# Context ahead of x, shared block sums, unstacked first maxima and products of zeros in the prologue of a gated cross-attention block

## The chip, the cores and the metric

One core of one Trainium2 chip runs the whole kernel. The metric is the device time in microseconds of one execution, as the median of several. TensorE multiplies, VectorE and ScalarE (ACT) work on its PSUM results, POOL (GpSimd) works on SBUF alone, and SyncE (SP), ACT and POOL issue the transfers. Each engine takes its own instructions strictly in order and waits on semaphores.

## The reference

The layer is computed for four batches of 512 rows and 512 columns, in fp32. `quant` below is per 1x128 block for the activations and per 128x128 block for the context.

```python
# attention to the context, as a product of two quantised matrices (fp8, with block scales)
x = x + tanh(g_xattn) * einsum('emk,enk->emn', quant_1x128(layernorm(x)), quant_128x128(ctx))
# causal self-attention, 16 heads of 32
h = layernorm(x)
fused = h @ (Wa * col_scale)          # 512 x 1536: q 24 + 8 tail, k 24 + 8 tail, v
q_tail, k_tail = where(w_rec > 0.1, swapped low-rank parts, low-rank parts)
attn = softmax(causal(q @ k.T / sqrt(32)))
x = x + tanh(g_ffn) * ((attn @ v) @ Wp)
```

## The kernel before

**Precision.** Each fp32 product is made of three fp32r products of high and low parts (hi hi, hi lo, lo hi), so a product of 512x512x128 takes 12 matmuls (L594 to L596). The quantised tiles are split into three fp8 parts and turned by 12 small products each (`turn_parts`, L610).

**Stages of a batch n.** Context: maxima over its blocks (`ctx_maximum`, t), two small transposes with the block scales (A, or B in the prologue for the next batch), POOL scales and clips (`scale_up`, s in the prologue, g in the body), ACT casts into fp8 parts (`cast`, C or c), TensorE turns (W). x: statistics (x), inverse deviation on POOL (i), normalisation (L), block maxima (F, or m), scales, again scale_up (u), cast (C) and turn (X). Then 16 block products (`partial_sum`, S, i is the row tile and k the block, number 4i+k), each added to x by VectorE with a scale of its own (`add_sum`, four operations of 128x128, L1201). Then second statistics (b), POOL's inverse deviation (r), ACT's normalisation (N), TensorE's turn (H), ACT's copy of the high part and VectorE's subtraction for the low part (H), and products q, k, v in four groups of heads (q0, k0, q1, k1, V0 to V3 or v3, Q2, K2, Q3, K3; a suffix .012 names the parts).

**The attention** runs in eight steps of two heads (u), software-pipelined: `max` (units 0 to 5, scores for the maxima of step u+1 on TensorE, L717, and masked maxima on VectorE, L1230), `rowmax` (L723, turns the maxima) with ACT's `neg` and a transfer into q_stack, `exp` (scores again, L734, and exponentials on ACT), POOL's `zero`, `pv` (values of step u-1, L748, which waits for the previous `norm` and for POOL), ACT's `copy`, TensorE's `back` (L757) and VectorE's `norm`. The rows of q and k, high and low, are stacked on 96 partitions by transfers (`stack_rows`, L345), so that one matmul makes all three products.

**What sets the order.** Every engine's order is written out by hand as strings of names: PE_STEPS, ACT_STEPS, DVE_STEPS, POOL_STEPS for batches 0 to 2, the _LAST strings for batch 3, the _END strings between batches and the _FIRST strings for the prologue. A name in a string is one piece on that engine; a piece late in one queue holds up everything behind it. `BEFORE` names the piece that must have freed a PSUM bank.

**The prologue** (the _FIRST strings) also prepares the weights: ACT rounds them (a, b), VectorE sorts the low-rank tails (T), POOL subtracts the rounded parts (j for q and k, l for v). q0 waits for all four j (`s_wlo`), v0 for all four l. The first x goes through `first_x`, which lies in qk_lo; the fourth part of the weights is loaded into qk_hi. SP loads x, then the context, then the weights. ACT issues eleven small transfers (gates, w_rec, col_root) before its first instruction. POOL_FIRST is `i0 s0 s1 ... s5 o0 s6 j0 s7 r0 j1 l0 l1 r1 l2 l3 r2 r3 j2 j3 ...`.

**Maxima of step 0.** They take the stacked rows: TensorE's M0 to M2 (two units each) wait for the transfers of q_stack and k_stack.

## Time and profile before

| | us |
|---|---|
| median of 3 runs | 502.21 |
| lowest, highest | 500.25, 502.68 |
| the profiled execution | 499.74 |
| its span, first to last instruction | 497.9 |
| TensorE busy | 440.6 (88%) |
| VectorE busy | 340.3 (68%) |
| ACT busy | 255.7 (51%) |
| POOL busy | 151.1 (30%) |

The span of the profiled execution is 1.8 us shorter than its time. The page's slices show TensorE filled from about 50 us on; the first 80 us are the prologue, then come four batches. Durations of matmuls are modelled to their ends and overlap, so the distance from one start to the next is the pace.

### The profile page before, as it was taken

To read this page: it belongs to the slowest core of one execution; us is meant where nothing else is said; L and a number is where in the kernel's file an instruction comes from. 1 tells how busy PE (TensorE), PEld (TensorE's weight loads), DVE (VectorE), ACT (ScalarE), POOL (GpSimd) and SP (SyncE) were. 2 spreads that over 40 slices of the span, in tenths; PEclk is the share of its full clock that TensorE was granted. 3 is DMA by queue.
4 is the path that set the end of the run, shared out by engine and by line. 5 is a ranking of instruction groups with operands and counts; after the bars stand their busy time and mean duration, and the time that the engine had idled before them with its cause. 6 is when DMAs were issued, how large, how long until landed. Compare 5 with 4: busy or idle time off the path is not lost.

```text
span 497.9 us, 7913 instructions
## 1 busy us (share of the span) xinstructions
PE 440.6 (88%) x2536; PEld 317.1 (64%) x2536; DVE 340.3 (68%) x1122; ACT 255.7 (51%) x498; POOL 151.1 (30%) x278
## 2 busy tenths in 40 slices
...
GB/s 225 197 1 87 39 246 82 91 69 96 146 2 2 89 101 193 67 56 95 141 27 0 64 97 127 138 53 98 97 11 2 58 102 97 64 95 102 60 21 86
DMA packets 27929, 42.62 MB, mean 86 GB/s; under 512 B 8272, under 2 KB 8528, under 8 KB 27888
## 3 DMA queue, kind: packets, MB, share of 16 engines
...
q0 software_dynamic: 192, 0.39, 0.3%
...
## 4 chain that ended last, share of the span: by engine, by line
PE 66%; DVE 24%; ACT 3%; issue 3%; DMA 2%; POOL 1%; SPq 0%; ACTq 0%; DVEq 0%; POOLq 0%
PE pv_bank L748 13%; DVE x_all L1201 10%; PE mm_bank L594 9%; PE mm_bank L595 8%; PE mm_bank L596 8%; PE exp_bank L734 6%; PE max_bank L717 5%; DVE max_bank L1230 5%; PE mm_bank L775 2%; PE mm_bank L777 2%; PE mm_bank L776 2%; PE turn_bank L610 2%; DVE bn L1208 2%; PE pv_bank L757 1%; DMA x_all<-in_x 1%
## 5 line engine op out<-in xcount | busy, mean ns | idle before, releaser
L1230 DVE CUSTOM_DVE_ANT_0 max_bank<-max_bank,causal 128x512 f32<-128x512 f32 (+3 forms) x256 | 121.0, 512 | 52.5 <-PE max_bank L717 52.0
L1002 ACT ACTIVATE work<-exp_bank 128x512 f32<-128x512 f32 (+1 forms) x192 | 94.9, 526 | 56.2 <-PE exp_bank L734 55.2
L512 POOL TENSOR_SCALAR_AFFINE_SELECT work<-work 128x384 f32<-128x384 f32 x64 | 33.4, 522 | 281.6 <-ACT work L1002 281.6
L748 PE MATMUL pv_bank<-work,v_aug 128*33 128x256 f32 (+3 forms) x512 | 78.9, 451 | 0.6 <-DVE work L1241 0.2
L734 PE MATMUL exp_bank<-q_stack,k_stack 97*128 97x512 f32 (+3 forms) x256 | 71.2, 341 | 7.6 <-ACT work L1002 6.5
L717 PE MATMUL max_bank<-k_stack,q_stack 96*128 96x512 f32 (+3 forms) x256 | 71.1, 338 | 2.4 <-DVE row_max L1230 1.8
L1201 DVE SCALAR_TENSOR_TENSOR x_all<-mm_bank,coef,x_all 128x128 f32<-128x128 f32 x224 | 61.5, 342 | 0.3
L748 PEld LDWEIGHTS pv_bank<-work,v_aug 128*33 128x33 f32 x512 | 29.7, 113 | 50.1 <-issue 42.1
L734 PEld LDWEIGHTS exp_bank<-q_stack,k_stack 97*128 97x128 f32 x256 | 45.6, 188 | 23.4 <-ACT work L1002 14.7
L594 PE MATMUL mm_bank<-xt_hi,w_hi 128*128 128x512 f32 x128 | 53.4, 417 | 0.7 <-ACT v_aug L981 0.7
L717 PEld LDWEIGHTS max_bank<-k_stack,q_stack 96*128 96x128 f32 x256 | 45.2, 191 | 12.7 <-DVE row_max L1230 3.7
L595 PE MATMUL mm_bank<-xt_lo,w_hi 128*128 128x512 f32 x128 | 50.3, 393 | 0.0
L596 PE MATMUL mm_bank<-xt_hi,w_lo 128*128 128x512 f32 x128 | 50.1, 392 | 0.0
L1213 DVE SCALAR_TENSOR_TENSOR qk_lo<-mm_bank,col_root,qk_hi 128x512 fp32r<-128x512 f32 x32 | 24.0, 749 | 34.0 <-ACT qk_hi L973 33.9
L973 ACT ACTIVATE qk_hi<-mm_bank,col_root 128x512 fp32r<-128x512 f32 x32 | 21.9, 686 | 32.6 <-PE mm_bank L596 32.6
L1230 DVE DVE_READ_ACCUMULATOR2_ANT row_max<- 128x1 f32 x256 | 36.1, 141 | 0.0
L996 ACT ACTIVATE values<-pv_bank 97x512 f32<-97x512 f32 x32 | 19.1, 598 | 27.4 <-PE pv_bank L748 27.4
L610 PE MATMUL turn_bank<-part_sign,tile_buf 128*128 128x128 fp8e4 x312 | 23.1, 227 | 5.4 <-ACT tile_buf L963 4.6
L642 PE MATMUL mm_bank<-wt_hi,wt_lo 128*128 128x512 f32 x56 | 23.3, 458 | 4.9 <-DVE x_all L1201 3.0
L596 PEld LDWEIGHTS mm_bank<-xt_hi,w_lo 128*128 128x128 f32 x128 | 24.0, 188 | 5.5
L594 PEld LDWEIGHTS mm_bank<-xt_hi,w_hi 128*128 128x128 f32 x128 | 24.2, 189 | 5.1 <-issue 1.2
L989 ACT ACTIVATE neg_max<-exp_bank 8x128 fp32r<-8x128 f32 x32 | 8.3, 260 | 35.5 <-PE exp_bank L723 35.5
...
## 6 DMA issues: line engine op xcount, KB each, us to landing
q_stack<-qk_hi SPq DMA_DIRECT2D x128, 64.0 KB, 2.0
...
```

The costliest lines, as they stand in the source:

```text
L512: pool.affine_select(out=three, in_=three, compare_op=ALU.is_ge, fill=0.0, base=0, pattern=[[0, 3], [1, P]], channel_multiplier=-1)
L594: pe.matmul(dst, l_hi(k), r_hi(k), start=(k == 0), stop=False)
L595: pe.matmul(dst, l_hi(k), r_lo(k), start=False, stop=False)
L596: last = pe.matmul(dst, l_lo(k), r_hi(k), start=False, stop=(k == NK - 1))
L610: last = pe.matmul(bank[:, P * k:P * k + P], part[:, P * k:P * k + P], part_sign[:, t, :], start=(t == 0), stop=(t == 2))
L717: last = pe.matmul(bank[:, col:col + width], q_stack[0:96, s, j, P * i:P * i + P], k_stack[0:96, s, j, 0:width], start=True, stop=True)
L734: last = pe.matmul(bank[:, col:col + T - P * i], k_stack[0:97, s, j, P * i:P * i + P], q_stack[0:97, s, j, P * i:T], start=True, stop=True)
L748: last = pe.matmul(pv_bank[64 * j:64 * j + D + 1, P * m:T], v_aug[:, m, 2 * u + j, :], prob[j][:, PROB_COL[m]:PROB_COL[m] + T - P * m], st ...
L1002: act.activation(prob[j][:, UNIT_COL[k]:UNIT_COL[k] + UNIT_LEN[k]], exp_bank[(3 * j + k) % 2][:, 0:UNIT_LEN[k]], ACT.Exp, scale=SCALE).the ...
L1201: last = dve.scalar_tensor_tensor(x_part, sum_bank(first, i, k)[:, P * t:P * t + P], coef[:, i, t, k:k + 1], x_part, ALU.mult, ALU.add)
L1213: dve.scalar_tensor_tensor(qk_lo[:, g % 2, w, :], mm_bank[w][:], col_root[:, g:g + 1], qk_hi[:, g % 2, w, :].bitcast(FP32), ALU.mult, ALU. ...
L1230: last = dve.tensor_tensor_reduce(max_bank[unit % 2][:, col:col + width], max_bank[unit % 2][:, col:col + width], causal[:, T - width:T], ...
```

## The change

It rewrites the prologue and puts the pieces of every step string into another order.

- SP loads the context before x; the fourth part of the weights comes in three pieces into other places (raw_v and raw_low early, raw_qk after the first j); the transfers of col_root are issued by SP behind the weights; ACT issues w_rec and the gates after its signs.
- `first_x` lies in v_aug; the maxima of first_x (F) are separate and the scales are made for two tiles at once (G).
- The context's turned parts are copied by VectorE (`first_ctx`, f) and not by ACT.
- Of the four block sums of a row tile, the fourth is multiplied by its scale on ACT (`first_product`, s) and added by POOL (a); VectorE adds three.
- Maxima of step 0 take q and k unstacked from qk_hi and qk_lo on 32 partitions, three matmuls for each product (`first_scores`), unit by unit.
- TensorE multiplies `causal[:, 0:384]`, which holds zeros, into exp_bank[1] (w0 to w11, four matmuls each).
- All step strings are in a new order, without a change to what is computed.

```diff
-    "max0 rowmax max1 S0 S1 pv max2 S2 max3 X1 max4 exp0 S3 back S4 exp1 exp2 S5 S6 max5 X2 exp3 exp4 exp5",
-    "rowmax max0 max1 S7 pv max2 max3 S8 S9 exp0 max4 exp1 back exp2 exp3 exp4 max5 X3 exp5 S10",
-    "S11 max0 rowmax max1 pv S12 max2 S13 max3 H0 S14 exp0 exp1 max4 exp2 H1 exp3 exp4 S15 exp5 max5 back",
-    "max0 rowmax max1 A0 pv exp0 H2 max2 exp1 exp2 max3 max4 exp3 exp4 max5 exp5 back",
+    "max0 X0 max1 rowmax S0 S1 max2 pv S2 max3 exp0 max4 S3 exp1 X1 back max5 exp2 S4 exp3 exp4 X2 exp5 S5 S6",
+    "max0 rowmax max1 S7 pv exp0 max2 S8 exp1 max3 exp2 max4 S9 X3 S10 exp3 exp4 max5 exp5 back",
+    "rowmax S11 max0 max1 S12 pv exp0 max2 S13 exp1 back max3 exp2 S14 H0 exp3 max4 exp4 max5 exp5 S15",
+    "H1 max0 rowmax max1 A0 pv exp0 max2 exp1 H2 exp2 max3 exp3 max4 exp4 max5 exp5 back",
...
-    "neg C1 copy X1 C2 exp0 exp1 exp2 exp3 exp4 exp5",
-    "neg X2 copy C3 exp0 exp1 exp2 exp3 exp4 exp5",
+    "neg C1 C2 copy exp0 X1 exp1 exp2 exp3 exp4 exp5",
+    "neg C3 X2 exp0 exp1 exp2 exp3 exp4 copy X3 exp5",
...
-    "K3 max0 max1 S0 S1 max2 max3 S2 S3 S4 norm max4 max5",
-    "b0 S5 max0 S6 S7 max1 b1 max2 S8 max3 max4 S9 norm max5",
-    "S10 max0 max1 S11 t0 S12 max2 max3 H0 S13 max4 S14 b2 S15 t1 t2 max5 t3 norm b3 H1",
-    "A0 max0 max1 max2 max3 max4 max5 H2 norm",
+    "max0 max1 S0 max2 S1 S2 max3 S3 max4 S4 max5 norm",
+    "S5 max0 S6 max1 S7 max2 S8 max3 max4 S9 max5 S10 norm b0",
+    "max0 b1 S11 max1 S12 t0 b2 max2 S13 max3 S14 max4 t1 max5 t2 H0 t3 S15 norm b3 A0",
+    "max0 H1 max1 max2 max3 max4 H2 max5 norm",
...
-PE_FIRST = ("f0 f1 f2 f3 f4 S0 S1 S2 S3 f5 S4 S5 S6 f6 S7 S8 f7 S9 f8 S10 S11 S12 S13 S14 "
-     "S15 f9 f10 v0 f11 v1 q0 B0 B1 k0 V2 q1 M0 k1 M1 M2")
+PE_FIRST = ("f0 w0 w1 f1 f2 w2 f3 f4 w3 S0 w4 S1 S2 f5 S3 S4 S5 w5 w6 w7 w8 S6 w9 S7 "
+     "f6 f7 S8 S9 S10 S11 S12 S13 f8 S14 S15 w10 w11 f9 v0 f10 v1.0 f11 v1.123 q0.0 B0 q0.12 B1 q0.3 "
+     "k0.012 V2 k0.3 q1.01 M0 q1.23 M1 k1.01 M2 k1.2 M3 k1.3 M4 M5")
...
+ACT_FIRST = ("a0 a1 C0 C1 C2 C3 C4 d0 b0 f4 C5 f5 b1 s0 C6 C7 f6 s1 f7 N0 a2 s2 b2 a3 "
+     "s3 e3 f8 N1 b3 f9 N2 v0 N3 f10 f11 q0 c0 v1 V2 k0 c1 D0 q1 c2 D1 p0 k1 c3")
...
+DVE_FIRST = ("t0 t1 t2 t3 w0 A0 x0 x1 A1 x2 x3 T0 L0 L1 F0 L2 T1 F1 F2 G0 f0 L3 f1 F3 "
+     "G1 f2 f3 c0 T2 S0 S1 S2 T3 S4 b0 S5 S6 S8 S9 b1 S10 S12 S13 S14 b2 h0 b3 u0 "
+     "h1 u1 u2 h2 u3 h3 B0 B1 q0 k0 M0 M1 q1 M2 M3 M4 M5 k1")
...
+POOL_FIRST = ("i0 s0 s1 s2 s3 s4 s5 s6 j0 s7 o0 a0 j1 r0 l0 a1 l1 l2 a2 r1 l3 a3 r2 r3 "
+     "j2 j3 v0 g0 g1 g2 D0 D1 g3 p0")
...
-    "PE": "Z1 Z2 pv Z3 back Z4 Z5 z3 Z6 Z7 Z8 Z9 Z10 Z11",
+    "PE": "pv Z2 back Z3 z3 Z4 Z5 Z6 Z7 Z8 Z9 Z10 Z11",
...
-        first_x = qk_lo[:].bitcast(FP32).rearrange("p g w t -> p (g w) t")
+        first_x = v_aug[:].rearrange("p i h e -> p i (h e)")[:, :, 0:C]
...
-            load_tiles(0, 0)
             load_ctx(0)
+            load_tiles(0, 0)
...
+                elif kind == "a":
+                    pool.wait_ge(s_fmul, i + 1)
+                    pool.wait_ge(s_summed, 3 * i + 3)
+                    pool.tensor_tensor(x_tile(0, i), x_tile(0, i), tile_buf[:, i, :], ALU.add).then_inc(s_fadd, 1)
...
+            def first_scores(unit):
...
+                if unit >= 2:
+                    pe.wait_ge(s_max, unit - 1)
+                rows = slice(D * j, D * j + D)
+                for i, col in MAX_UNITS[k]:
+                    width = P * (i + 1)
+                    dst, cols = max_bank[unit % 2][:, col:col + width], slice(P * i, P * i + P)
+                    pe.matmul(dst, qk_hi[rows, 0, 0, cols], qk_hi[rows, 0, 1, 0:width], start=True, stop=False)
+                    pe.matmul(dst, qk_lo[rows, 0, 0, cols], qk_hi[rows, 0, 1, 0:width], start=False, stop=False)
+                    last = pe.matmul(dst, qk_hi[rows, 0, 0, cols], qk_lo[rows, 0, 1, 0:width], start=False, stop=True)
+                last.then_inc(s_sm, 1)
...
+                elif kind == "w":
+                    for _ in range(4):
+                        pe.matmul(exp_bank[1][:, 0:T - P], causal[:, 0:P], causal[:, 0:T - P], start=True, stop=True)
...
+            def first_product(i):
+                act.wait_ge(s_coef, 1)
+                act.wait_ge(s_turn, i + 1)
+                act.wait_ge(s_cross, NK * i + NK)
+                for t in range(NT):
+                    last = act.activation(tile_buf[:, i, P * t:P * t + P], sum_bank(True, i, NK - 1)[:, P * t:P * t + P],
+                                          ACT.Copy, scale=coef[:, i, t, NK - 1:NK])
+                last.then_inc(s_fmul, 1)
...
+            def first_ctx(p):
+                dve.wait_ge(s_turn, p + 1)
+                dve.tensor_copy(wt_hi[:, :, P * p:P * p + P],
+                                first_bank(p)[:].rearrange("p (k c) -> p k c", k=NK)).then_inc(s_fctx, 1)
```

## Rows read from the trace of the kernel before

**Rows 1.** The page, part 1: busy time of each engine over the span.
```profile
PE 440.6 (88%) x2536; PEld 317.1 (64%) x2536; DVE 340.3 (68%) x1122; ACT 255.7 (51%) x498; POOL 151.1 (30%) x278
```
**Rows 2.** Windows: stretch, busy per engine (instructions), clock, DMA share, GB/s.
```profile
3.00:4.00 1.00, 0.00 (x0) 0.00 (x0) 0.00 (x0) 0.00 (x0) 1.00 (x1) 1.00 0.67 144
...
8.00:9.00 1.00, 0.00 (x0) 0.00 (x0) 0.83 (x2) 0.36 (x2) 0.00 (x0) 1.00 1.07 392
```
**Rows 3.** Timeline (start, length, operation), first 30 us; last, a transfer's landing.
```profile
8.61 0.69 DVE L1139 BATCH_NORM_STATS2 bn<-x_all 128x6 f32<-128x512 f32 x1 [0.17 <-DMA x_all<-in_x]
...
11.60 1.00 DVE L1156 TENSOR_SCALAR qk_lo<-x_all,shift,rstd 128x512 f32<-128x512 f32 x2 [0.72 <-POOL rstd L473]
...
13.94 0.37 PE L618 MATMUL turn_bank<-ident,w_amax 128*16 128x128 f32 x1 [13.94 <-DVE w_amax L1114]
...
16.08 1.04 POOL L505 TENSOR_TENSOR tile_buf<-ctx_raw,w_up 128x512 f32<-128x512 f32 x1 [4.51 <-DVE w_down L1125]
...
19.84 1.46 PE L610 MATMUL turn_bank<-part_sign,tile_buf 128*128 128x128 fp8e4 x12 [4.62 <-ACT tile_buf L963]
...
27.98 3.59 DVE L1149 SCALAR_TENSOR_TENSOR coef<-x_down,gates,w_down 128x16 f32<-128x16 f32 x4
...
x_all<-in_L_ffn_w_rec ACTq DMA_DIRECT2D x1, 8.0 KB, 3.8
```
**Rows 4.** Timeline from 30 to 59 us: block sums on VectorE, POOL's queue.
```profile
31.68 2.36 DVE L1201 SCALAR_TENSOR_TENSOR x_all<-mm_bank,coef,x_all 128x128 f32<-128x128 f32 x8
...
49.50 2.15 DVE L1201 SCALAR_TENSOR_TENSOR x_all<-max_bank,coef,x_all 128x128 f32<-128x128 f32 x8
...
52.68 0.23 POOL L471 TENSOR_SCALAR shift<-mv 128x1 f32<-128x1 f32 x1 [3.20 <-DVE mv L1209]
...
54.06 1.85 POOL L528 TENSOR_TENSOR w_lo<-work,w_hi 128x768 fp32r<-128x768 f32 x1
...
56.56 1.85 POOL L528 TENSOR_TENSOR w_lo<-qk_hi,w_hi 128x768 fp32r<-128x768 f32 x1
```
**Rows 5.** Timeline and chain from 59 to 81 us: products, a transfer, maxima, first turn.
```profile
59.70 0.39 PE L594 MATMUL mm_bank<-xt_hi,w_hi 128*128 128x512 f32 x1
...
63.40 0.20 PE L621 MATMUL turn_bank<-ident,tile_buf 16*128 16x16 f32 x1 [0.71 <-DVE tile_buf L1131]
...
70.84 2.50 DMA k_stack<-qk_lo
...
73.58 0.70 PE L717 MATMUL max_bank<-k_stack,q_stack 96*128 96x512 f32 x3 [0.61 <-DMA k_stack<-qk_lo]
...
80.08 0.83 PE L610 MATMUL turn_bank<-part_sign,tile_buf 128*128 128x128 fp8e4 x12
```
**Rows 6.** Timeline of batch 0's body: K3's low part, end of step 5, chain's pv.
```profile
110.51 0.75 DVE L1213 SCALAR_TENSOR_TENSOR qk_lo<-mm_bank,col_root,qk_hi 128x512 fp32r<-128x512 f32 x1
...
144.52 0.37 PE L723 MATMUL exp_bank<-ident,row_max 128*8 128x128 f32 x1 [3.09 <-DVE row_max L1230]
...
145.54 3.30 PE L748 MATMUL pv_bank<-work,v_aug 128*33 128x512 f32 x16
...
168.59 2.28 PE pv_bank L748 x16
```
**Rows 7.** Windows in v0's stretch and behind the pause of step 5.
```profile
54.00:55.00 1.00, 1.00 (x4) 0.81 (x3) 1.00 (x2) 0.85 (x2) 1.00 (x2) 0.50 0.00 0
...
145.00:146.00 1.00, 0.99 (x5) 0.33 (x6) 0.96 (x3) 0.19 (x1) 0.00 (x0) 0.50 0.00 0
```
**Rows 8.** The chain that ended last, one matmul of v1 at full clock.
```profile
58.04 0.23 PE exp_bank L595
```
**Rows 9.** Groups by form: busy us, mean ns, idle before.
```profile
L537 POOL TENSOR_TENSOR w_lo<-work,w_hi 128x512 fp32r<-128x512 f32 x3 | 3.8, 1284 | 0.0
...
L963 ACT ACTIVATE tile_buf<-ctx_raw 128x512 fp8e4<-128x512 f32 x28 | 17.2, 614 | 0.0
...
L989 ACT ACTIVATE neg_max<-exp_bank 8x128 fp32r<-8x128 f32 x32 | 8.3, 260 | 35.5 <-PE exp_bank L723 35.5
```

More of the change, by code:

```diff
@@ L107 @@
     "max0 max1 max2 max3 max4 max5",
[1 row of a table removed]
[1 row of a table added]
     "max0 K2 max1 max2 max3 norm max4 max5",
[4 rows of a table removed]
-    "norm",
-]
-PE_FIRST = ("f0 f1 f2 f3 f4 S0 S1 S2 S3 f5 S4 S5 S6 f6 S7 S8 f7 S9 f8 S10 S11 S12 S13 S14 "
-     "S15 f9 f10 v0 f11 v1 q0 B0 B1 k0 V2 q1 M0 k1 M1 M2")
-ACT_FIRST = ("a0 C0 C1 C2 f0 d0 f1 C3 f2 C4 b0 f3 f4 C5 C6 f5 a1 C7 f6 b1 f7 N0 f8 a2 "
-     "a3 N1 f9 N2 b2 f10 N3 b3 v0 f11 v1 q0 k0 c0 V2 D0 c1 p0 q1 D1 k1 c2 c3")
-DVE_FIRST = ("x0 w0 x1 x2 x3 t0 t1 L0 L1 t2 t3 L2 A0 A1 T0 F0 F1 L3 F2 F3 T1 T2 c0 S0 "
-     "S1 S2 S3 b0 S4 S5 S6 S7 S8 b1 S9 S10 S11 S12 b2 S13 h0 S14 S15 b3 T3 h1 u0 u1 "
-     "h2 u2 h3 u3 B0 q0 B1 k0 M0 q1 M1 M2 k1")
@@ L127 @@
-POOL_FIRST = ("i0 s0 s1 s2 s3 s4 s5 o0 s6 j0 s7 r0 j1 l0 l1 r1 l2 l3 r2 r3 j2 j3 g0 g1 "
-     "D0 g2 D1 g3 p0")
-PE_END = "pv k1.3 V0.012 max0 back V0.3 max1 V1.01 y0 max2 y1 V1.2 max3 V1.3 V2.0 max4 V2.123 max5 y2 y3 O0 O1 O2 O3"
-ACT_END = "q1 k1 copy V0 y0 V1 y1 c2 V2 y2 c3 y3"
-DVE_END = "k1 norm max0 max1 max2 max3 y0 max4 y1 max5 y2 O0 y3 O1 O2 O3"
[5 rows of a table added]
+]
+PE_FIRST = ("f0 w0 w1 f1 f2 w2 f3 f4 w3 S0 w4 S1 S2 f5 S3 S4 S5 w5 w6 w7 w8 S6 w9 S7 "
+     "f6 f7 S8 S9 S10 S11 S12 S13 f8 S14 S15 w10 w11 f9 v0 f10 v1.0 f11 v1.123 q0.0 B0 q0.12 B1 q0.3 "
+     "k0.012 V2 k0.3 q1.01 M0 q1.23 M1 k1.01 M2 k1.2 M3 k1.3 M4 M5")
@@ L136 @@
+PE_END = ("q1.23 k1.012 pv V0.0 k1.3 V0.12 back V0.3 V1.0 max0 y0 y1 V1.1 max1 V1.2 max2 V1.3 V2.0 max3 V2.1 max4 V2.23 max5 y2 "
+     "y3 O0 O1 O2 O3")
+ACT_END = "q1 copy k1 c1 y0 V0 y1 c2 V1 c3 V2 y2 y3"
+DVE_END = "k0 q1 k1 norm max0 max1 max2 y0 y1 max3 max4 max5 y2 O0 O1 y3 O2 O3"
 END_LAST = {
-    "PE": "Z1 Z2 pv Z3 back Z4 Z5 z3 Z6 Z7 Z8 Z9 Z10 Z11",
+    "PE": "pv Z2 back Z3 z3 Z4 Z5 Z6 Z7 Z8 Z9 Z10 Z11",
     "ACT": "copy z3",
-    "DVE": "z2 Z1 Z2 norm Z3 z3 Z8 Z9 Z10 Z11",
+    "DVE": "Z1 norm Z2 Z3 z3 Z8 Z9 Z10 Z11",
@@ L703, in side, with scores_for_max @@
                     qk_product("QK".index(kind), i, ks)
-            def scores_for_max(n, u, j, k, first=False):
+            def first_scores(unit):
+                j, k = unit // 3, unit % 3
+                if unit == 0:
+                    pe.wait_ge(s_const, 3)
+                    pe.wait_ge(s_summed, 12)
+                    pe.wait_ge(s_fmul, NT)
+                    pe.wait_ge(s_qklo, 2)
+                if unit >= 2:
[8 more added lines that the diff above has]
+                last.then_inc(s_sm, 1)
+            def scores_for_max(n, u, j, k):
                 s, unit = u % SLOTS, 3 * j + k
@@ L711, in scores_for_max @@
                         pe.wait_ge(s_pstack[s], 48)
-                if unit >= 2 or not first:
-                    pe.wait_ge(s_max, 48 * n + 6 * u + unit - 1)
+                pe.wait_ge(s_max, 48 * n + 6 * u + unit - 1)
                 bank = max_bank[unit % 2]
```

179 lines of the change are left out of this document (102 added, 77 removed), and 73 rows, old and new, of tables (ACT_LAST, ACT_STEPS, BEFORE, BEFORE_LATE).

## The prediction

> **What bounds the kernel now.** I read the page first: TensorE is busy 440.6 of 497.9 us, VectorE 340.3 [rows 1]. Such an average hides the limits of stages, so I read the timeline, cut at the row-maximum transposes of L723, which open each step, and asked which engine is continuous there.
>
> The prologue has two stages. Until the last block sum of batch 0 (49.50 us and 2.15 for the last eight operations, so 51.65) VectorE is the limit: its sums start at 31.68 and come every 1.03 us, four operations each, with only statistics between. POOL subtracts the weights' high parts meanwhile; its last two pairs, j2 and j3, take 2.5 us each from 54.06, so the q product can start at 59.1 [rows 4]. Then TensorE is the limit from 59.70 to the body's first turn at 80.08 us: five products of 12 matmuls, the turns of the next context, six maxima units [rows 5].
>
> In the body TensorE has hardly any idle time except while the block sums of the next batch run. There VectorE's queue is the limit: K3's low part starts at 110.51 us, and at 144.52 TensorE has waited 3.09 us for VectorE's `max5` of step 5. `pv`, 2.28 us elsewhere, then takes 3.30 [rows 6]: the granted clock is 0.50 (1.2 of 2.4 GHz) behind the idle time [rows 7]. The next two batches repeat this; the last has no such stage.
>
> **The change, part by part.**
>
> *Loads and first scales.* Context is loaded ahead of x; of the ACT queue's small transfers eight go to SP's queue behind the weights, three behind ACT's signs. While they are issued the engines move 144 GB/s (3 to 4 us), later 392 [rows 2]. At these rates context is in by 6 to 8.5 us, x by 8.3 to 12. But VectorE's queue has `w0` ahead of the context transposes, and the row it needs now leaves ACT only after the first constants, a table load and the signs, at an estimated 4.4, and lands 3.8 later: 8.2. From there: w0 0.3; transposes and scales 2.1 (13.94 to 16.08), of which 0.7 runs beside a statistic; three statistics 2.1; the last one with aggregates and POOL's `i0`, which stands before `s0`, 3.0 (8.61 to 11.60) [rows 3]. So s0 starts at 15.0 and not 16.08, 1.1 us sooner. Ends: 13.0, were only the landings to count, and 16.5; I take what the queue order forces.
>
> The Trainium skill, "DMA: Bandwidth & Descriptors", section "Issuing engines are not separate DMA queues", says that starting transfers from another engine saves only issue time. By it the move gives context and x no bandwidth, s0 starts near 15.9, and the gain below would be 0.9 us smaller.
>
> *Zeros on TensorE.* Twelve groups of four products of 384 zero columns. A product of 512 repeats every 0.23 us at full clock [rows 8], so a group takes 0.65 us, at half clock 1.3. Twelve fp8 turn products take 1.46 us at 19.84 and 0.83 at 80.08 [rows 3, 5]: TensorE starts out at half speed. Nine products of v0 fall in a stretch granted 0.50 [rows 7], 0.2 us more each, 1.8 us. The zeros may cure both, but the groups before f1 delay it: C0 ends at 18.9, f0 at 20.3, w0 and w1 at 22.9, f1 at 24.3. VectorE, which makes the context copies now, waits for f1 from 21.8 on; then come copies, F3, G1, four coefficients (3.6 [rows 3]) and T2, and the first sum starts at 32.7, 1.0 us later than before. With a clock that stays low it is 33.6, without the wait 31.2; I take 32.7, half warm.
>
> The Trainium skill, "TensorE: Matmul & The Clock Gate", section "What's actually happening", calls the throttled state the default and activity what releases it. The 1.46 us agrees; the column of the granted clock, which says 1.00 at that place, does not. Were the column right, zeros would only cost, about 1 us more than in the sum.
>
> *Shared sums.* VectorE loses four sums, 4.1 us, and two of four scale chains, and gains four copies, 0.6 each as the 128x512 forms of ACT [rows 9]. ACT gets 16 products of 128x128: below, 0.26 each, an 8x128 form; above, 0.61, a form of 512 columns; 0.28 taken, near the lower as 128 columns go with it; 4.5 us, beside waits for TensorE. POOL gets four additions of 128x512: 1.04 as L505, or 1.28 as L537 [rows 3, 9]; 1.04, since the types are those of L505.
>
> Now POOL's queue decides. `a0` waits for S2, at 32.7 + 3 x 1.03 = 35.8. Behind it stand a0 to a3 (4.2), r0 to r3 (1.4 each, 52.68 to 54.06), l0 to l3 (1.28 each) and j1, j2, j3 (2.5 each) [rows 4, 9]: 4.2 + 5.6 + 5.1 + 7.5 = 22.4, so q0 may start at 58.2. I walked a1, a2, a3 against S6, S10, S14 (about 41, 45, 48 us): no further wait. With 0.3 for semaphores 58.5, against 59.70: gain 1.2 us. TensorE has v1 done at about 57 and waits 1.5; that VectorE is finished sooner is worth only this, as q0 waits for weights. It is also what hides the moved `e3`, `s` and T3.
>
> *Unstacked maxima.* Before, 59.70 to 80.08 is 20.4 us, with idle time of 0.7 at the context transposes, 0.6 for a stacked row's transfer and more behind V2 and among the maxima [rows 5]. After: 60 products at 0.23, 13.8; transposes 0.6; 7680 columns of maxima at 0.23 per 512, 3.45; small waits 0.6: 18.4. The maxima's bounds: 0.23, a product's pace, and 0.39, one alone [rows 5, 8], 5.9; the first, as they stand back to back. But `D1` in ACT's queue now stands behind q1 and c2 (c2, three casts of 0.61, 1.9 [rows 9]): its last transfer leaves at 75.8, lands 2.5 later [rows 5] at 78.3, and `max0` of step 0 wants it at 77.6. Gain: 20.4 - 18.4 - 0.7 = 1.3.
>
> *The body's order.* TensorE's instructions are the same. In the VectorE-bound stretch I asked what VectorE does before it releases TensorE. Before, that is all up to `max5` of step 5: sums S0 to S15, statistics, t0 to t2, H0. After, TensorE's H1 stands ahead of the transpose and waits for VectorE's H0: the same work without S15, 1.03 us less. But `pv` waits for norm, and norm now stands behind S15. So pv starts as before; only H1's low part now stands behind `max0`. Bounds 0 and 1.03 per batch; I take 0.2, near the bound that the queue gives, three batches, 0.6. TensorE's pause ahead of H1 is again near 3 us, so the clock falls again. K3, S10, A0 and the contexts' POOL pieces move inside the same continuous queue: 0; uncovered, each costs its length, 0.5 to 1.7. The last batch is bound by TensorE: order only, 0; z3 has only Z3, six products, 1.4 us, over norm, which is enough.
>
> Sum: -1.2 -1.3 -0.6 = -3.1. The profiled execution took 499.74, 2.47 below the median of 502.21; so 496.6 for such a one and 499.1 as the median.
>
> **Rivals.**
>
> (1) *More is won*: the transfers and zeros do all they can (first sum at 31.2, 1.5 us), and TensorE's pause splits between H1 and pv so that the clock stays, 1.0 us of pv in each of three batches [rows 6]. 499.1 - 4.5 = 494.6. For it: the pause has two parts now. Against: the first is as long as before.
>
> (2) *The gain cancels*: a low clock through the zeros (0.9), POOL's additions at 1.28 (1.0), D1 1 us later: 502.0. For it: POOL works in order and has no slack after a0.
>
> (3) *Slower*: in step 4 ACT's `copy` moves behind exp4 and TensorE's `back` to the end; VectorE's norm, and behind it b0, b1, N0 and H0, wait for it. I find back done 0.6 us before norm's turn. It decides once exp4 comes more than 0.6 us later than I have it, say behind a late transfer of the negated maxima; every further microsecond is lost where VectorE has no slack. 2.6 us late gives 2 us in three batches: 505.1. Against: TensorE reaches step 4 sooner, as C2 no longer holds up exp0 in step 3.
>
> (4) *The change does not do what it says*: the zeros leave v0 at half clock. Its 2.4 us are covered by 1.5 of waiting for weights: 500.0, inside the main case.
>
> **How the numbers follow.** Main case with (4): 0.50, 497.5 to 501.5. Rival 1: 0.22, 492 to 497. Rival 2: 0.15, 501 to 503.5. Rival 3: 0.13, 503 to 507. The range leaves out the far ends of 1 and 3: 493.0 to 504.5. A difference of 0.5% is 2.5 us, about what a measurement of this kernel can tell from no change: the line is at 499.7. Faster: 0.22 and 0.29 of the main case, 0.51. Slower, above 504.7: 0.12 with some drift. Same: 0.37.
>
> **What would show it.** s0 near 15 us; fp8 turns at 0.83 us from about 25 us on; granted clock 1.00 from 45 to 56 us; first sum at 32.7; POOL's last subtraction ending at 58.5 with the q product at once behind it and TensorE idle ahead; first transpose L723 near 77.5; the first `max0` of the body waiting for a k_stack transfer; the batches as far apart as before within 1 us, with about 3 us of idle TensorE before H1's turn and a clock of 0.50 behind it. Wrong would be: VectorE and not POOL last before q0; batches more than 1 us closer or farther; norm waiting for L757 in step 4.

## The result and the profile after

The changed kernel took 502.45 us in the median of 20 runs (499.83 to 505.47), the kernel before 501.19 us in the same series. The ratio is 1.0031, 95% interval 1.0017 to 1.0045: 1.6 us slower (1.3 by the two medians), which is less than the 0.5% that I had taken as the line, but away from zero. I had forecast 3.1 us faster. The ratios leave out slow executions, of which the 20 programs measured here had one, 844.72 us in before_again. The profiled execution of the changed kernel took 502.57 us with a span of 500.8; before it was 499.74 and 497.9.

Part 1 of the page of the changed kernel (busy us, share, instructions), against [rows 1]:

```profile
PE 445.0 (89%) x2600; PEld 319.0 (64%) x2600; DVE 338.7 (68%) x1102; ACT 256.8 (51%) x510; POOL 155.6 (31%) x282
```

Each sum hides what happened, so I cut both timelines at the same five places: s0 (GpSimd's first scale), S (VectorE's first block sum), q0 (the first query product), the first row-maximum transpose, and the first one of the last batch. For the changed kernel (start, length, operation, idle time and its cause):

```profile
15.05 0.24 POOL L486 TENSOR_SCALAR shift<-mv 128x4 f32<-128x4 f32 x1 [8.65 <-DVE mv L1196]
...
16.85 1.03 POOL L520 TENSOR_TENSOR tile_buf<-ctx_raw,w_up 128x512 f32<-128x512 f32 x1
...
34.17 2.15 DVE L1258 SCALAR_TENSOR_TENSOR x_all<-mm_bank,coef,x_all 128x128 f32<-128x128 f32 x8
...
62.82 0.47 PE L613 MATMUL mm_bank<-xt_hi,w_hi 128*128 128x512 f32 x1 [1.48 <-POOL w_lo L543]
...
83.11 0.84 PE L629 MATMUL turn_bank<-part_sign,tile_buf 128*128 128x128 fp8e4 x12
...
84.12 0.27 PE L763 MATMUL exp_bank<-ident,row_max 128*8 128x128 f32 x1 [0.17 <-DVE row_max L1290]
```

The rows of before are 16.08, 31.68, 59.70, 80.08 [rows 3 to 5]. So s0 comes 0.8 us later, S 1.7 later behind s0, q0 0.6 later behind S: 3.1 us lost at q0. From q0 to the body's first turn it is 20.29 against 20.38. The five stages of all the executions that I profiled (worked out from rows like these; us):

| kernel | s0 | s0 to S | S to q0 | s0 to q0 | q0 to first transpose | to last batch's | last batch |
|---|---|---|---|---|---|---|---|
| before | 16.08 | 15.60 | 28.02 | 43.62 | 20.27 | 332.06 | 85.87 |
| before_again | 16.27 | 15.60 | 27.73 | 43.33 | 20.37 | 334.73 | 85.60 |
| last_on_before | 16.45 | 15.62 | 27.59 | 43.21 | 20.57 | 334.17 | 85.10 |
| new_body | 16.27 | 15.60 | 27.58 | 43.18 | 20.00 | 334.40 | 84.55 |
| nb_j2 | 16.05 | 15.62 | 27.90 | 43.52 | 20.05 | 333.81 | 84.87 |
| nb_j2_w | 16.13 | 15.61 | 29.51 | 45.12 | 19.77 | 333.27 | 84.81 |
| **changed** | 16.85 | 17.32 | 28.65 | 45.97 | 21.30 | 332.09 | 84.59 |
| no_zeros | 15.41 | 17.31 | 28.29 | 45.60 | 21.34 | 332.74 | 84.61 |
| no_mid_zeros | 17.26 | 17.33 | 28.28 | 45.61 | 21.31 | 333.58 | 84.64 |
| j1_first | 16.09 | 17.31 | 27.26 | 44.57 | 21.31 | 333.14 | 84.59 |
| old_body | 16.40 | 17.33 | 28.58 | 45.91 | 21.66 | 333.65 | 85.18 |
| t3_late | 17.56 | 15.95 | 29.33 | 45.28 | 21.18 | 333.04 | 84.64 |
| stacked_max | 17.15 | 17.33 | 28.76 | 46.09 | 23.05 | 333.30 | 84.61 |
| add_on_vector | 17.80 | 17.31 | 29.58 | 46.89 | 21.19 | 333.40 | 84.62 |
| x_first | 17.12 | 17.05 | 28.32 | 45.37 | 21.32 | 331.66 | 84.63 |
| x_j1_t3 | 17.80 | 15.66 | 30.78 | 46.44 | 21.27 | 332.56 | 84.63 |
| ctx_on_act | 16.37 | 14.74 | 27.51 | 42.25 | 21.29 | 334.15 | 84.64 |
| stage_old | 17.36 | 16.77 | 28.35 | 45.12 | 20.15 | 335.75 | 84.62 |
| best | 16.84 | 15.76 | 27.61 | 43.37 | 19.89 | 333.48 | 84.72 |
| best_nz | 17.63 | 15.46 | 27.95 | 43.41 | 20.14 | 334.84 | 84.68 |

The stages between s0 and the transpose repeat within some 0.6 us where nothing in them was edited, with one exception: up to S, best has the strings of ctx_on_act and takes 15.76 us against 14.74 (the reason stands under best). s0 scatters by 2.4 us and the long stretch to the last batch by 4, so one trace settles nothing there.

### The profile page after: what moved, and what is told of

Same layout as the page of the kernel before. It is cut to its first block, busy times and chain, and to the rows that moved or that the text cites. A ratio compares the mean times of both kernels' runs of the same rounds, so it can differ in the third digit from the quotient of the medians.

```text
span 500.8 us, 8055 instructions
## 1 busy us (share of the span) xinstructions
PE 445.0 (89%) x2600; PEld 319.0 (64%) x2600; DVE 338.7 (68%) x1102; ACT 256.8 (51%) x510; POOL 155.6 (31%) x282
## 4 chain that ended last, share of the span: by engine, by line
PE 62%; DVE 17%; ACT 3%; POOL 3%; issue 2%; DMA 1%; POOLq 0%; ACTq 0%
PE pv_bank L788 11%; PE mm_bank L613 9%; PE mm_bank L614 8%; PE mm_bank L615 8%; DVE x_all L1258 8%; PE exp_bank L774 5%; DVE max_bank L1290 5%; PE max_bank L757 5%; PE mm_bank L815 2%; PE mm_bank L817 2%; PE mm_bank L816 2%; PE turn_bank L629 2%; DVE bn L1268 1%; PE pv_bank L797 1%; DMA q_stack<-neg_max 1%
## 5 line engine op out<-in xcount | busy, mean ns | idle before, releaser
L527 POOL TENSOR_SCALAR_AFFINE_SELECT work<-work 128x384 f32<-128x384 f32 x64 | 33.4, 521 | 275.8 <-ACT work L1036 275.8
L788 PE MATMUL pv_bank<-work,v_aug 128*33 128x256 f32 (+3 forms) x512 | 77.0, 443 | 0.7 <-POOL work L530 0.3
L757 PE MATMUL max_bank<-k_stack,q_stack 96*128 96x512 f32 x248 | 71.0, 338 | 2.9 <-DVE row_max L1290 2.9
L774 PEld LDWEIGHTS exp_bank<-q_stack,k_stack 97*128 97x128 f32 x256 | 44.8, 189 | 15.9 <-ACT work L1036 6.8
L664 PE MATMUL mm_bank<-wt_hi,wt_lo 128*128 128x512 f32 x56 | 24.8, 463 | 9.1 <-DVE x_all L1258 7.2
```

The lines of the kernel that those rows point to most:

```text
L527: pool.affine_select(out=three, in_=three, compare_op=ALU.is_ge, fill=0.0, base=0, pattern=[[0, 3], [1, P]], channel_multiplier=-1)
L664: pe.matmul(sum_bank(first, i, k)[:], wt_lo[:, k, P * i:P * i + P], wt_hi[:, k, 0:C], start=True, stop=True).then_inc(s_cross, 1)
L757: last = pe.matmul(bank[:, col:col + width], q_stack[0:96, s, j, P * i:P * i + P], k_stack[0:96, s, j, 0:width], start=True, stop=True)
L774: last = pe.matmul(bank[:, col:col + T - P * i], k_stack[0:97, s, j, P * i:P * i + P], q_stack[0:97, s, j, P * i:T], start=True, stop=True)
L788: last = pe.matmul(pv_bank[64 * j:64 * j + D + 1, P * m:T], v_aug[:, m, 2 * u + j, :], prob[j][:, PROB_COL[m]:PROB_COL[m] + T - P * m], st ...
```

## The experiments

### Zeros, GpSimd's order, the body's order

```
no_zeros:      PE_FIRST without w0 ... w11
no_mid_zeros:  -S5 w5 w6 w7 w8 S6 w9 S7   +S5 S6 S7
j1_first:      POOL_FIRST -o0 a0 j1 r0 l0 a1   +o0 j1 a0 l0 r0 a1
old_body:      strings of body and last batch, and their tables, as before
```

**no_zeros.** 

> The changed kernel with none of the twelve groups of zero products in its prologue (w0 to w11); everything else as changed. Theory A (GpSimd's queue sets the first query product q0, and behind the context coefficients VectorE's queue sets the block sums, so TensorE's clock between them is worth little): first block sum on VectorE within 0.7 of the changed kernel's 34.17 us, q0 within 0.7 of 62.82, the whole 501.5 to 503.2 against 502.45. Rival B (the zeros stand in the way of block sums and hold q0 back): S6 comes 2 us or more sooner, q0 near 60.5, the whole near 500. Rival C (the zeros buy what they were put in for): the context turns at half clock, first sum 1 us or more later, value products f9 to v1 at half clock, q0 at 64 to 65, the whole near 504.

Measured: 1.0042 [1.0026, 1.0058], as slow as the changed kernel. S stands 17.31 us behind s0, with zeros 17.32. Without zeros the fp8 turns take 1.46 and 1.44 us throughout the start; with them they fall to 0.83 from 25.21 on:

```profile
21.03 1.46 PE L629 MATMUL exp_bank<-part_sign,tile_buf 128*128 128x128 fp8e4 x12 [0.40 <-ACT tile_buf L997]
...
23.53 1.44 PE L629 MATMUL turn_bank<-part_sign,tile_buf 128*128 128x128 fp8e4 x12 [1.04 <-DVE wt_hi L1314]
```

```profile
20.63 1.44 PE L629 MATMUL turn_bank<-part_sign,tile_buf 128*128 128x128 fp8e4 x12 [9.77 <-ACT tile_buf L997]
...
25.21 0.83 PE L629 MATMUL turn_bank<-part_sign,tile_buf 128*128 128x128 fp8e4 x12
```

The first fence is no_zeros, the second the changed kernel. The zeros raise the clock, as meant, and in this prologue nobody waits for it: theory A held for the distances. In absolute times S (32.72) and q0 (61.01) fell outside its 0.7 us, because s0 came 1.44 us sooner. The margin is thin: without zeros TensorE is ready only 0.20 us before GpSimd, with them 1.48.

**no_mid_zeros.** 

> The changed kernel without the zero groups w5 to w9 alone (those between the sums S5, S6 and S7, 20 products at half clock in its trace). Theory A (GpSimd's queue sets q0, and this queue stood for a sum of block 1 for 0.30 us at the most): S6 on TensorE 2 to 4 us sooner, but q0 within 0.5 of 62.82, the whole 501.9 to 502.9. Rival B (S6 held back holds everything): q0 2 us or more sooner, the whole near 500.

Measured: 1.0055 [1.0039, 1.0070]; s0 to q0 45.61 against 45.97. Theory A on the stage; the whole is 1.2 us outside its window, which only the scatter outside the edited stage is there to explain. Holding back S6 isn't the cause.

**j1_first.** 

> The changed kernel with one change of order on GpSimd: the low weight part j1 (1.86 + 0.77 us) ahead of the addition a0, and l0 (1.28) ahead of r0, so that this work falls into the 2.03 us and 1.36 us in which GpSimd's queue stood at a0 for the third sum and at r0 for VectorE's statistics. Theory A: what GpSimd does not wait comes off q0: a0 at 38.1 instead of 37.50, q0 at 60.0 to 61.0 instead of 62.82, the whole about 2 us shorter, near 500.4. Rival B (something else is just behind GpSimd): q0 no sooner than 62.2, the whole within 0.7 of the changed kernel.

Measured: s0 to q0 44.57, 1.0 to 1.4 us less than the 45.6 to 46.0 of its neighbours, and TensorE waits 0.24 us for GpSimd instead of 1.48. The whole is 1.0048 [1.0023, 1.0073], no sooner. GpSimd is the last before q0, but TensorE's value products are 0.24 us behind it: eight of them took 0.63 us in this trace, zeros and all. A was right on the engine and half right on the size.

**old_body.** 

> The changed kernel with the orders of the body and of the last batch (the strings of all four engines and the tables of the time before which a step may be taken) put back to those of the kernel before; prologue, transfers, zeros and unstacked first maxima stay changed. Theory A (the traces put 3.1 us of loss on q0, nothing on the body between the first row-maximum transposes and the last batch, and 1.3 us of gain on the last batch): q0 at 62.8, last batch 85.9 instead of 84.6, the whole 1.0 to 1.6 us slower than the changed kernel, near 503.8. Rival B (the new orders of the body are what loses): the whole sooner than the changed kernel, under 501.5. Rival C (the orders don't matter): within 0.4 of the changed kernel.

Measured: 1.0081 [1.0056, 1.0106], 2.5 us slower than the changed kernel by the ratios. The body's orders help; they aren't the loss.

### One step of the chain at a time

```
t3_late:        DVE_FIRST -c0 T2 S0 S1 S2 T3 S4 b0 S5 S6   +c0 S0 S1 S2 S4 b0 S5 T2 S6 T3
stacked_max:    PE_FIRST  ... q1 M0 k1 M1 M2, two units each, from q_stack and k_stack
last_on_before: kernel before with PE_LAST, ACT_LAST, DVE_LAST, END_LAST, BEFORE_LAST of the changed one
add_on_vector:  a0 a1 a2 a3 from POOL_FIRST to DVE_FIRST
```

**t3_late.** 

> The changed kernel with VectorE's turns of the low weight parts later: T2 behind S5 and T3 behind S6, instead of ahead of S0 and of S4. In the four runs of the changed prologue so far the first block sum began 17.31 to 17.33 us after GpSimd's first scale s0 (before 15.60), with zeros and without. Theory A (VectorE's queue makes that 17.3: T2 is 2.05 us in front of S0, T3 3.4 us in front of S4, both beside GpSimd): s0 to first sum 15.2 to 16.2, a0 on GpSimd 1 us or more sooner against s0 and no 1.36 us wait at r0 (s0 to q0 44 or less instead of 45.6 to 46.0), the whole 1 to 2 us shorter. Rival B (the coefficients or a turned tile come last there): s0 to first sum over 16.8, the whole unchanged.

Measured: s0 to S 15.95, as theory A has it, but s0 to q0 45.28 and 1.0042 [1.0024, 1.0060]. Whatever is taken from in front of the sums comes back between them: GpSimd now waits 1.69 us for VectorE at a2 (49.26). So VectorE's whole queue up to its last sum counts, not the place of one item. TensorE was as late as GpSimd here: it reached q0 without idle time, with six value products at 0.63 us.

**stacked_max.** 

> The changed kernel with the first head pair's scores for the maximum computed again from the stacks, two units after each product (M0 behind q1, M1 behind k1, M2), as the kernel before does; all else changed. Theory A (the unstacked form costs what it was to win: three products of 32 rows for one of 96, 4.7 us for 24 of them and their changes of form): q0 to the first row-maximum transpose 20.3 to 20.8 instead of 21.3, the whole 0.5 to 1 us shorter. Rival B (the forecast's step: the wait for the stacks and for their transfer, 0.61 us in the kernel before, and the maxima behind the products are what was saved): 22 to 23 us there, the whole 1 us or more longer.

Measured: 23.05 us and 1.0107 [1.0085, 1.0130]. Rival B: in this order of products the stack's transfer comes last, and the unstacked form is worth 1.75 us in this stage (the whole lost 3.8 us by the ratios; where the rest went isn't shown):

```profile
78.64 0.70 PE L758 MATMUL max_bank<-k_stack,q_stack 96*128 96x512 f32 x3 [3.39 <-DMA k_stack<-qk_lo]
```

Before, the same wait was 0.61 us [rows 5].

**last_on_before.** 

> The kernel before with the order of the last batch (and its tail behind the last step, and the table of times for it) of the changed kernel, nothing else. Theory A (that order gained 1.28 us in the trace of the changed kernel, from 85.87 to 84.59, and has nothing to do with the prologue): from the first row-maximum transpose of the last batch to the end 84.4 to 84.9, the whole 1.0 to 1.3 us faster than before, ratio 0.9975 or so. Rival B (those 1.28 us come from the rest of the change, as a state of the buffers that the new body leaves): no more than 0.3 us, ratio 1.000.

Measured: 85.10 us in the last batch, ratio 1.0006 [0.9991, 1.0020]. Neither theory: the stage is 0.5 to 0.8 us shorter than in the two traces of the kernel before, and the whole shows nothing of it.

**add_on_vector.** 

> The changed kernel with the four additions of the scaled fourth tile product (a0 to a3, 1.26 to 1.30 us each on GpSimd) on VectorE instead, each in front of the next block's sums. Theory A (GpSimd's queue sets q0): GpSimd loses 5.1 us of work and its waits at a0; VectorE gains four times 0.67 (its row for a 128x512 subtraction) and loses the 1.04 us in which it stood for a3. Then VectorE's last low part is what q0 waits for: s0 to q0 44 to 44.8 instead of 45.6 to 46.0, the whole 1 to 1.8 us shorter. Rival B (VectorE was as late as GpSimd): s0 to q0 45.5 or more, the whole unchanged or longer.

Measured: s0 to q0 46.89, 1.0078 [1.0050, 1.0107]. Rival B, plainly. An addition takes 0.68 to 0.77 us on VectorE against 1.28, and GpSimd then stands 2.90 and 3.54 us for VectorE's statistics. With j1_first this says: relieve GpSimd and q0 moves 1.2 us; load VectorE with 2.8 us and it moves back 0.9 us. Here too TensorE was the last at q0, with five value products at 0.63 us, so the 0.9 us isn't VectorE's alone.

### Load order, and the orders of the body alone

```
x_first:      -load_ctx(0); load_tiles(0, 0)   +load_tiles(0, 0); load_ctx(0)
              DVE_FIRST  +x0 w0 x1 x2 x3 t0 t1 L0 L1 t2 t3 L2 A0 A1 T0 F0 T1 F1 ...
x_j1_t3:      x_first, j1_first and t3_late together
new_body:     kernel before with all body, end and last-batch strings and tables of the changed one
before_again: kernel before, unchanged
```

**x_first.** 

> The changed kernel with the loads of x ahead of those of the context again, and VectorE's first steps in the matching order (statistics of x first, context maxima between the norms); everything else as changed. Theory D, new: in the changed trace VectorE works without a break from the first norm of x (16.91) to the first block sum (34.17), and that norm waits for GpSimd's i0, which waits for the last x tile (statistics end 14.89, i0 1.8 us) - i0 is also ahead of s0 in GpSimd's queue, while the context's scales lay ready at 13.29. So the context ahead of x has put off VectorE's chain. Then here i0 starts near 10, s0 near 16, and the first block sum at 31.0 to 32.3 instead of 33.4 to 34.6 (s0 to first sum under 16), q0 1 to 2.5 us sooner than the 62.3 to 62.9 of the changed kernel, the whole 1 to 2 us shorter. Rival E (the turned context and its copies set the first sum): first sum no sooner than 33.4.

Measured: i0 at 10.95 and the norms early, yet s0 17.12, S 34.17, 1.0044 [1.0029, 1.0058]. Theory D fell: bringing x first takes three norms from between s0 and S, and S doesn't move, since T0 now lies behind s0, and it and T1 fell beside GpSimd's scales (1.05, 1.00 and 1.13 us for pieces that take 0.3 elsewhere in this trace). Rival E's number held, not sooner than 33.4. Nor does the load order alone explain the late s0.

**x_j1_t3.** 

> The changed kernel with three edits together: x loaded first (as in x_first), GpSimd's j1 ahead of a0 and l0 ahead of r0 (as in j1_first, which took 1.2 us off s0 to q0), VectorE's T2 and T3 behind S5 and S6 (as in t3_late, which took 1.37 us off s0 to the first sum). If the three are one chain after the other (theory A with D), first sum near 30.5, q0 at 57.5 to 59, the whole 3 to 4.5 us under the changed kernel, and under the kernel before by 1 to 3 us. If the value products and their norms are close behind (rival), q0 at 59.5 to 61, the whole no better than the kernel before.

Measured: 1.0087 [1.0072, 1.0102]; s0 to q0 46.44, the three gains did not add up. GpSimd no longer waits at a0 or r0, but 1.01 us at a1 and 2.92 us at a2, both for VectorE's sums.

**new_body.** 

> The kernel before with the body orders, the batch ends and the last batch of the changed kernel (strings of all four engines and the tables), its own prologue and stacked first maxima kept. The last batch's order alone gave 1.0006 on this kernel. Theory A (body and last batch together are worth something only as a set; old_body lost 2.5 us against the changed kernel by ratio, 1.0081 against 1.0031): 1.0 to 2.5 us faster than before, ratio 0.995 to 0.998. Rival (the new orders fit only the changed prologue): ratio 0.999 or more.

Measured: 499.20 us against 500.61, ratio 0.9972 [0.9956, 0.9989]. Theory A. These orders gain 1.4 us where the prologue is left alone: this version beats both kernels.

**before_again.** 

> The kernel before, unchanged, to see how far the stages of one profiled execution vary: so far s0 lay between 15.41 and 17.80 in eight traces of the changed prologue and at 16.08 and 16.45 in two of the old one, and the time from the first to the last batch's row-maximum transpose between 332.1 and 334.2. Expected: ratio 1.000 within 0.0015; s0 to first sum 15.6, s0 to q0 43.2 to 43.6, q0 to the first row-maximum transpose 20.3 to 20.6, the last batch 85.1 to 85.9. If the last batch shows 85.1, most of the 1.28 us that the changed kernel seemed to gain there was the one execution.

Measured: 1.0008 [0.9993, 1.0023], stages as expected, last batch 85.60. The stretch to the last batch was 334.73, 2.7 us more than in the trace from which I predicted. Of the 1.28 us that the changed kernel gains in the last batch some 0.3 was the one trace.

### The two open causes, and the best of both

```
ctx_on_act:  DVE_FIRST -f0 -f1 -f2 -f3   ACT_FIRST +a0 a1 C0 C1 C2 g0 d0 g1 C3 g2 C4 b0 g3 f4 ...
             (g: the copy of first_ctx as act.activation(..., ACT.Copy))
stage_old:   stacked_max, and q0 B0 B1 k0 V2 q1 M0 k1 M1 M2 on TensorE, with ScalarE's,
             VectorE's and GpSimd's strings from q0 on as before
nb_j2:       new_body, POOL_FIRST -r3 j2 j3   +j2 r3 j3
nb_j2_w:     nb_j2 with 18 zero products between S12 and v0
best:        ctx_on_act and stage_old;   best_nz: best without zero products
```

**ctx_on_act.** 

> The changed kernel with the four copies of the turned context (f0 to f3, 0.60 to 0.68 us each) on ScalarE instead of VectorE, between its casts, as the kernel before has them. Theory F (VectorE's queue sets the first sum: between its first norm and the first sum it has 0.5 us idle at the most): s0 to the first sum falls from 17.3 to 14.7 to 15.6, q0 against s0 1 to 2 us sooner than 45.6 to 46.0, the whole 1 to 2 us shorter than the changed kernel. Rival G (ScalarE's casts, in whose queue the copies now stand, hold the x tiles back as much): s0 to first sum 16.5 or more, the whole unchanged.

Measured: s0 to S 14.74, s0 to q0 42.25 against 45.97, ratio 0.9992 [0.9973, 1.0010] against 1.0031. Theory F. The windows from VectorE's first norm to its first sum (stretch, then busy us of TensorE, its weight loads, VectorE, ScalarE, GpSimd), of the changed kernel and of this one:

```profile
16.91:34.17 17.26, 10.95 (x96) 7.61 (x96) 16.91 (x30) 14.24 (x28) 16.12 (x19) 1.00 0.14 32
```

```profile
16.43:31.11 14.68, 8.58 (x80) 6.00 (x81) 14.18 (x26) 13.77 (x26) 13.89 (x16) 1.00 0.12 38
```

VectorE is busy 16.91 of 17.26 us. Four copies of 0.7 us went, and 2.58 us of the stretch with them; ScalarE, with 3 us free, took them for nothing. The stretch is one trace of each; in best the same edit gave 1.56 us.

**stage_old.** 

> The changed kernel with the whole stage from q0 to the body as the kernel before has it: scores for the first maxima from the stacks, whole products q0, k0, V2, q1, k1, and the orders of ScalarE, VectorE and GpSimd around them. In stacked_max the form alone was put back and q0 to the first row-maximum transpose grew from 21.3 to 23.05; the kernel before has 20.3 to 20.6 there, new_body 20.00. Theory H (the unstacked form wins against its own order, but that order, with V2 ahead of k0 on ScalarE and five changes between products and maxima, costs what it wins): 20.0 to 21.0 here, the whole 0.3 to 1.3 us shorter than the changed kernel. Rival I (both parts of the new stage are worth having): 21.5 or more, the whole longer.

Measured: 20.15 us in the stage, theory H; but 1.0030 [1.0009, 1.0051] on the whole, so the 1.15 us don't show there. Its stretch to the last batch was the longest of all, 335.75 us; whether by chance I can't say.

**nb_j2.** 

> The kernel before with the changed kernel's body and last batch orders (new_body, 0.9972) and GpSimd's low part j2 (1.85 + 0.7 us) ahead of r3, in the 3.2 us in which GpSimd stood there for VectorE's statistics. Its last low part then ends near 56.8 instead of 59.3. Theory (TensorE, which runs from v0 to q0 without a pause at half clock, is the bound there and GpSimd is 0.3 us behind it): q0 within 0.4 of new_body's 59.45, ratio 0.996 to 0.998. Rival (GpSimd is the bound): q0 near 58.5, ratio 0.995.

Measured: q0 at 59.57, ratio 0.9976 [0.9958, 0.9993]. The theory: on the old prologue TensorE is the bound there.

**nb_j2_w.** 

> nb_j2 with six groups of three zero products between the last sums and v0 (w4 behind S12, w5 behind S13, w0 ahead of and w1 behind S15, w2 and w3 behind f9), 18 in all, written to the bank that only v0 uses next. In new_body TensorE idles 2.5 us ahead of f10 and computes v0 and the start of v1 at half clock. Theory (with GpSimd's queue out of the way, clock is worth something): full clock from v0 on, q0 at 57.9 to 58.8, ratio 0.994 to 0.997. Rival (x1's norms of the last tile, N3 and f11, hold v1): v0 shorter, v1 and q0 no more than 0.3 sooner, ratio as nb_j2.

Measured: 0.9992 [0.9971, 1.0014], q0 at 61.25. Worse than either theory by the stage, 1.7 us; the interval of the ratio overlaps that of nb_j2. v0 did run at full clock (50.86 to 53.7); then TensorE had little to do until v1 at 56.85, where seven of twelve products took 0.63 us, at half clock, instead of 0.39. The zeros moved the slow stretch from v0, which is covered, to v1, which isn't.

**best.** 

> The changed kernel with ctx_on_act and stage_old together: context copies on ScalarE, and the stage from q0 to the body as the kernel before has it; load order, shared sums, zeros and body orders stay changed. If the two causes add up: q0 at 42.3 behind s0 (58.3 to 59.5), first row-maximum transpose 20.15 behind q0, at 78.5 to 79.7 against 79.97 before, body and last batch as the changed kernel: ratio 0.995 to 0.997. If they don't (the earlier q0 only meets a later wait for the stacks): first row-maximum transpose at 80.5 or later, ratio 0.999 or more.

Measured: 500.36 us, 0.9984 [0.9967, 1.0001]. First transpose at 80.10 with s0 at 16.84: 63.26 us behind s0, where the changed kernel has 67.27 and before 63.89. Alone, ctx_on_act had given 3.72 us up to q0 and stage_old 1.15 behind it; together they give 4.01 and not 4.87, and q0 comes 43.37 behind s0, not 42.3. The whole stops short of the 0.995 to 0.997 expected, and isn't better than new_body. The first two of these rows are of best, the third is ctx_on_act's for the turn of the first:

```profile
24.41 1.49 PE L629 MATMUL exp_bank<-part_sign,tile_buf 128*128 128x128 fp8e4 x12
...
32.60 2.16 DVE L1268 SCALAR_TENSOR_TENSOR x_all<-mm_bank,coef,x_all 128x128 f32<-128x128 f32 x8 [2.57 <-PE mm_bank L664]
```

```profile
23.42 0.83 PE L629 MATMUL exp_bank<-part_sign,tile_buf 128*128 128x128 fp8e4 x12
```

In best the eight zero products ahead of this turn took 2.76 us (2.20 in ctx_on_act), the turn itself 1.49. ScalarE, which has the copies now, waited 1.09 us for it, and VectorE 2.57 us for TensorE's first block product. So once the copies are off VectorE's queue, the first sum hangs on TensorE, and the zeros and the clock that they find count for about 1 us there, which differs from execution to execution.

**best_nz.** 

> best without the zero products. Theory (where VectorE's queue is not the bound, clock is): value products v0 and v1 at half clock in part, q0 1 to 2 us later against s0 than in best (over 43.3), the whole 1 to 2 us longer than best. Rival (the zeros buy nothing anywhere, as in no_zeros): q0 within 0.4 of best's against s0, the whole within 0.6 us of best.

Measured: s0 to q0 43.41 against 43.37, 0.9994 [0.9975, 1.0013]. The rival. In best_nz TensorE stood at half clock from 34 to 50 us, in best it mostly did not:

```profile
34.00:50.00 16.00, 12.36 (x53) 7.92 (x52) 13.88 (x52) 12.60 (x32) 13.96 (x19) 0.50 0.31 93
```

```profile
34.00:50.00 16.00, 12.93 (x79) 7.45 (x76) 14.18 (x51) 13.39 (x33) 14.99 (x21) 0.89 0.30 92
```

```profile
60.21 0.47 PE L613 MATMUL mm_bank<-xt_hi,w_hi 128*128 128x512 f32 x1 [1.48 <-POOL w_lo L543]
```

The first fence is best_nz, the second best; the third is best's q0, which waits 1.48 us for GpSimd, where TensorE in best_nz reaches q0 without idle time. So from S on the clock's gain ends in that wait; and up to S best is the later one, 15.76 against 15.46.

## Why the prediction was wrong, by its own steps

**The failed steps.** In the forecast's own terms q0 was to start at 58.5 and started at 62.82, 4.3 us late. Of that s0 is 1.85 (16.85 against 15.0), the distance to S -0.4, S to a0 0.2, and GpSimd's queue from a0 to q0 2.6 (25.3 against 22.7), the largest. The stage behind q0 took 20.29 and not 19.1 (18.4 and D1's 0.7), 1.2 more; the orders gave 1.4 and not 0.6. That is 4.7 us in sum, the distance from -3.1 to +1.6. That it closes so well is in part luck, as s0 alone scatters by 2.4 us.

**s0 at 15.0.** Missed, the first failing step. It is 16.85, and 16.89 in the mean of the 12 traces that load context first (15.41 to 17.80), against 16.21 in the mean of the 6 of the old prologue (16.05 to 16.45). I let x land at the rates of [rows 2]. With the small transfers out of the way they began faster (303 GB/s at 2 to 4 us, before 141) and then moved less (stretch, busy us per engine, clock, DMA share, GB/s):

```profile
6.00:8.00 2.00, 0.00 (x0) 0.00 (x0) 0.69 (x1) 0.00 (x0) 0.35 (x2) 1.00 0.44 131
8.00:10.00 2.00, 0.37 (x1) 0.09 (x1) 0.83 (x3) 0.00 (x0) 0.00 (x0) 1.00 0.64 191
```

Before it is 392 GB/s at 8 to 9 us [rows 2]. The Trainium skill ("DMA: Bandwidth & Descriptors", "Issuing engines are not separate DMA queues") said that starting transfers from another engine saves issue time only; no bandwidth was gained, that much holds, though s0 came later than the 15.9 that I had worked out for this case. And `i0` still stands ahead of s0: it starts at 15.05, when the context's scales had lain ready since 13.3. Putting s0 ahead of i0 wasn't tried, nor were the small transfers put back on ScalarE's queue, so why s0 is late stays open.

**First sum at 32.7.** The distance from s0, 17.7 by my working, measured 17.3, for the wrong reason. I had VectorE wait for f1 on TensorE and so gave the clock 0.9 us either way. no_zeros shows that TensorE's clock sets nothing there. ctx_on_act shows what does: VectorE's queue, in which the change puts four copies. My distance held these copies, so they aren't what the forecast missed by. But I had set them against the four lost sums, and the sums lie behind S, the copies ahead of it; with the wait put on TensorE I didn't see that they cost what they take. Without them the whole is no slower than before (0.9992).

**Zeros.** In the changed trace they warm the clock, as hoped: fp8 turns 0.83 us, v0's products 0.39 (granted 1.00 from 42 us), though from 34 to 42 us the clock was down again (0.61 and 0.53). Rival 4 is out for this trace. It isn't certain in every execution: in four others with all zeros (j1_first, t3_late, add_on_vector, ctx_on_act) five to eight value products took 0.63 us, and TensorE was idle for 0 to 0.48 us ahead of q0 instead of 1.4 to 1.5. What TensorE gains there ends in its wait for GpSimd: no_zeros, best_nz. The Trainium skill ("TensorE: Matmul & The Clock Gate", "What's actually happening") has activity lift the clock, and 1.44 to 0.83 agrees.

**POOL's queue, 22.4 us behind a0.** Right on the engine, short in two terms. a0 started at 37.50, 3.33 behind S (I had 3.1), and q0 came 25.3 later, not 22.7. The additions took 1.28, not 1.04: 1.0 us. And POOL waits 1.36 at r0 and 0.30 at a1, where I had walked the queue and found none:

```profile
37.50 1.26 POOL L571 TENSOR_TENSOR x_all<-x_all,tile_buf 128x512 f32<-128x512 f32 x1 [2.03 <-DVE x_all L1258]
...
42.67 0.25 POOL L486 TENSOR_SCALAR shift<-mv 128x1 f32<-128x1 f32 x1 [1.36 <-DVE mv L1269]
...
45.67 1.29 POOL L571 TENSOR_TENSOR x_all<-x_all,tile_buf 128x512 f32<-128x512 f32 x1 [0.30 <-ACT tile_buf L1051]
```

What r0 waits for is VectorE's statistics, which stand behind T3; and T3 I had called hidden:

```profile
37.59 1.33 DVE L1323 COPY_PREDICATED x_all<-x_all 128x128 f32<-128x128 uint32 x1
38.84 1.90 DVE L1324 COPY_PREDICATED x_all<-x_all 128x128 f32<-128x128 uint32 x1
```

**Unstacked maxima, -2.0 + 0.7.** The wait at max0 for D1's transfer didn't come. The stage from q0 to the first turn has TensorE busy without a gap:

```profile
62.82:83.11 20.29, 20.28 (x86) 14.38 (x87) 6.46 (x20) 11.45 (x18) 11.82 (x16) 1.00 0.67 201
```

Before it is 17.34 busy of 20.38. So the idle 3.0 us went, as forecast, and 2.9 us of work took its place. The maxima take 4.7 us from start to start (0.86, 0.99, 0.55, 0.90 and 1.41 for the last two), not 3.45. Another 1.2 us is left above 60 products at 0.23 and 0.6 of transposes: where the form changes, a product's record is 0.47 to 0.50 us long instead of 0.39 or 0.40. Against the stacked form in the new order they win 1.75 us (stacked_max), against the old form in the old order they lose 1.15 (stage_old) or 1.41 (best).

**Body, -0.6, and last batch, 0.** The pause ahead of H1 is 3.19 us with the clock at 0.50 behind it, as predicted. The size can't be read from one trace: unchanged strings gave 332.1 and 334.7. In the last batch I missed 0.3 to 1.3 us: with all the new orders it takes 84.55 to 84.87 in 16 traces, with the old ones 85.18 to 85.87 in 3. Together new_body puts the orders at -1.4 us, more than my 0.6; old_body, on the changed prologue, puts them at -2.5.

**The account.** Orders -1.4 (new_body); the rest of the change is then 1.6 + 1.4 = +3.0 where I had -2.5 (+4.1 with old_body's -2.5). Of it the context copies are 2.0 by the ratios (0.9992 against 1.0031, give or take 1.2 by their intervals), s0 about 0.7 by the means above. The stage from q0 costs 1.15 in the traces, which the whole didn't show. Of my rivals the second, that the gain cancels, came nearest (502.0); of its three mechanisms only the additions at 1.28 were real. Rival 3, a late norm in step 4, didn't occur: the batches are as far apart as before. Two slips of the working move nothing in the sum: four products of 384 columns are 0.69 us at 0.23 per 512, not 0.65, and v0's loss is 1.8 us in one place and 2.4 in another.
